# A graph kernel: first gathering in short-format passes, large counts found from the edge list, second root in another space

## The reference, cut to what matters

```python
def rgcn_gate_layer(x, row, col, edge_type, basis, att, gate_w, root, bias):
    w = jnp.einsum('rb,bio->rio', att, basis)          # 2 relations from 30 bases
    x_j = x[col]
    for r in range(2):
        gate = sigmoid(x_j @ gate_w[r, :, 0]); msgs.append(gate[:, None] * x_j @ w[r])
    msg = where(edge_type == 0, msgs[0], msgs[1])
    return segment_sum(msg, row) + x @ root + bias
h   = relu(rgcn_gate_layer(x, ..., basis1, ..., root1, bias1))
out = rgcn_gate_layer(h, ..., basis2, ..., root2, bias2)
```

## Time and profile before

| what | value |
|---|---|
| three timed runs | 1160.33, 1154.93, 1164.74 us; median 1160.33 |
| profiled execution | 1161.15 us; span of its trace 1159.4 us |
| mean granted TensorE clock | 0.985 of full speed |
| busy share of the span | PE 94%, DVE 72%, ACT 48%, POOL 48% |

### The profile page before, as it was taken

The page is one execution under the profiler, slowest core; times in us unless marked ns, Lnnn a source line. Parts: engine busy times, 40 slices in busy tenths (PEclk is TensorE's granted clock), DMA queues, the critical chain, the costliest instruction groups (busy, mean ns, idle before and its releaser), DMA issues. The chain is left out here.

```text
span 1159.4 us, 15448 instructions
## 1 busy us (share of the span) xinstructions
PE 1086.1 (94%) x4410; PEld 607.0 (52%) x4442; DVE 835.8 (72%) x1852; ACT 558.3 (48%) x978; POOL 559.3 (48%) x518
## 2 busy tenths in 40 slices
PE   3989888899999989899999999999999999999997
PEld 1564222344557453655565565555555557446664
DVE  5694677769755153688788788788888867849997
ACT  0221321310332221477777777777777744116663
POOL 1960112233433330667876666666666300027774
PEclk9988989999999999899999999999999999999999
DMA  7995997657211005595554454445454010026665
GB/s 283 341 404 212 360 400 264 231 184 233 84 48 46 13 14 194 132 259 111 114 110 92 101 98 95 100 95 97 98 98 88 1 55 23 9 93 197 203 206 173
DMA packets 60182, 172.66 MB, mean 149 GB/s; under 512 B 12645, under 2 KB 13189, under 8 KB 52552
## 3 DMA queue, kind: packets, MB, share of 16 engines
q0 software_dynamic: 31536, 72.01, 26.6%
q1 hardware_dynamic: 28568, 99.66, 23.4%
HBM read 159.65 MB, written 11.98 MB: 148 GB/s over the span
## 5 line engine op out<-in xcount | busy, mean ns | idle before, releaser
L1664 PE MATMUL PS<-wide,hidT 128*128 128x512 f32 x672 | 302.1, 592 | 2.2 <-DVE hidT L1540 0.4
L705 POOL DMA_INDIRECT rec_scratch<-rec_src,slot_row x84 | 102.5, 1220 | 252.8 <-DMA rec_scratch<-rec_src,slot_row 208.2
L1664 PEld LDWEIGHTS PS<-wide,hidT 128*128 128x128 f32 x672 | 128.6, 191 | 122.8 <-issue 120.5
L1482 POOL DMA_INDIRECT pair_sum<-table_j,counts_rec x84 | 136.7, 1627 | 27.3 <-issue 25.3
L1598 ACT ACTIVATE wide<-PS 128x512 f32<-128x512 f32 x168 | 100.5, 598 | 99.6 <-PE PS L1648 63.5
L1801 POOL DMA_INDIRECT u_space<-table_j,wide x87 | 86.1, 990 | 108.7 <-DMA table_j<-agg_space 81.8
L1474 POOL DMA_INDIRECT pair_sum<-table_i,counts_rec x84 | 89.5, 1066 | 98.9 <-PE PS L1648 59.5
L1603 ACT ACTIVATE wide<-wide,two 128x512 f32<-128x512 f32 x168 | 120.9, 720 | 6.2 <-DVE wide L1533 6.2
L1533 DVE SCALAR_TENSOR_TENSOR wide<-wide 128x512 f32<-128x512 f32 x168 | 116.4, 693 | 5.8
L1491 POOL DMA_INDIRECT rec_scratch<-rec_src,slot_row x84 | 89.5, 1066 | 40.9 <-issue 21.6
L1608 ACT ACTIVATE wide<-wide 128x512 f32<-128x512 f32 x168 | 105.8, 630 | 5.3
(11 more groups left out here) (325 smaller groups left out, 1884.9 us busy)
## 6 DMA issues: line engine op xcount, KB each, us to landing
pieces<-basis_rows SPq DMA_DIRECT2D x56, 1024.0 KB, 7.5
ring<-basis_low SPq DMA_DIRECT2D x30, 256.0 KB, 6.4
w_scratch<-pieces SPq DMA_DIRECT2D x112, 32.0 KB
counts_rec<-rec_scratch SPq DMA_DIRECT2D x1, 2856.0 KB, 9.8
rec_scratch<-rec_src,slot_row POOLq DMA_INDIRECT x168, 2.3
root<-L_gnn_root SPq DMA_DIRECT2D x2, 1024.0 KB, 8.0
rows_in<-in_rows_in SPq DMA_DIRECT2D x2, 1024.0 KB, 13.9
w_rel<-w_scratch SPq DMA_DIRECT2D x1, 2048.0 KB, 11.6
```

The costliest lines, as they stand in the source:

```text
L705: nc.gpsimd.indirect_dma_start(out=rec3_dram, out_offset=bass.IndirectOffsetOnAxis(ap=slot_row[:, 1, t:t + 1], axis=0), in_=rec, in_offset ...
L1482: nc.gpsimd.indirect_dma_start(out=pair_sum[:, t % GOT3, :], out_offset=None, in_=tables[0][1], in_offset=bass.IndirectOffsetOnAxis(ap=idx ...
L1664: m = nc.tensor.matmul(o, hidT[:, t % 2, k * P:(k + 1) * P], w2[:, k, :], start=False, stop=(k == KT - 1), skip_group_check=True)
```

## The change

Four things are done; the diff is cut to its core.

- **The first gathering** takes `counts_short` and two roundings of the gated rows, `first_hi` and `first_lo`, in 100 short multiplications instead of 50 full ones, with `rest` corrections as in the second gathering. ACT rounds the rows (`first_high`) and the counts (`counts_rounded`) during `Y0_LATE`; DVE does `split_block(0)`, `(1)` and `first_low` right after the last `unpack`.
- **The blocks with large counts** are found in the sort stage, from how many edges go from group to group: DVE copies the group marks (`both_kinds`), PE multiplies them (`pair_sums`, `block_sums`), DVE sums them and finds the numbers (`sums_of_groups`, `sums_of_blocks`, both `heavy_blocks`). The maxima over the counts are gone.
- **root2** is loaded into the space of the first weights (`w_rel[0]`), before most of the low blocks, and `root_rows` stands before Y1. `w_ij` goes to the place after Y1.
- **DVE's order**: `records` moves from the count stage to tile 40 of the sort stage; the bias additions and ten `sum2` move before the last `unpack`.

```diff
+            root = pieces[:, 4 * RING1 + 2:4 * RING1 + 2 + KT, :]
+            first_hi = nc.alloc_sbuf_tensor_at("first_hi", [P, 2 * NT, D], F32R, offset=packed_at)
+            root2 = w_rel[0][:, 0, :, :]
+            first_rows = pieces[:, FIRST_SLOT:FIRST_SLOT + 2 * NT, :]
+            first_lo = pieces_short[:, FIRST_SLOT:FIRST_SLOT + 2 * NT, :]
+            FIRST_HIGH_AT = 6
+            ROUNDED_PER = {7: 2, 8: 4, 9: 4}
-            SUM2_BEFORE_H1 = (16, 11, 11, 11, 11)
+            SUM2_EARLY = 10
+            SUM2_BEFORE_H1 = (6, 6, 6, 6, 6)
+            PAIR_SUMS_AT, BLOCK_SUMS_AT = 20, 50
...
 PE:
-                def gathered_first(c):
-                    for m_ in range(NT):
-                        if c == 0:
-                            pe.wait_ge(sem("counts"), 2 * NT + m_ + 1)
-                        for r in range(2):
-                            m = nc.tensor.matmul(PS[:, c, :], counts[r][:, m_, c * P:(c + 1) * P], y_first(r, m_),
-                                                 start=(m_ == 0 and r == 0), stop=(m_ == NT - 1 and r == 1))
-                    m.then_inc(sem("o0_mm"), 1)
+                def gathered_first(c, terms):
+                    for m_, r, part in terms:
+                        pe.wait_ge(sem("counts_short"), 2 * m_ + r + 1)
+                        pe.wait_ge(sem("first_lo" if part is first_lo else "first_hi"), 2 * m_ + r + 1)
+                        m = nc.tensor.matmul(PS[:, c, :], counts_short[r][:, m_, c * P:(c + 1) * P], part[:, first_at(r, m_), :],
+                                             start=((m_, r, part) == FIRST_TERMS[0]), stop=((m_, r, part) == FIRST_TERMS[-1]), skip_group_check=True)
+                    return m
+                def pair_sums():
+                    pe.wait_ge(sem("src_group"), 3)
+                    for g in range(ET // SUM_TILES):
+                        m = nc.tensor.matmul(PS[0:SUM_ROWS, SUMS_BANK, 0:2 * SUM_ROWS]..., dst_group[:, g, :, :]..., src_group[:, :, :, tiles], ...)
+                def block_sums():
+                    pe.wait_ge(sem("group_sums"), 4)
+                    for k in range(NT):
+                        m = nc.tensor.matmul(PS[0:1, SUMS_BANK, 2 * NT * k:2 * NT * (k + 1)], own_group[:, k:k + 1], group_sums, ...)
...
+                pe.wait_ge(sem("heavy_at"), 2)
+                rest_chunk = [rest_numbers(j, 8, NT - 1) for j in range(2)]
+                rest_first = [rest_numbers(j, 12, 2 * NT - 1) for j in range(2)]
                 for n in Y0_LATE:
...
-                    gathered_first(c)
+                pe.wait_ge(sem("rests"), 2)
+                for c in range(NT):
+                    gathered_first(c, FIRST_TERMS[:1])
+                pe.wait_ge(sem("first_hi"), 2 * NT)
+                pe.wait_ge(sem("first_lo"), 2 * NT)
+                for j in range(2):
+                    rest(rests[:, j, :], rest_chunk[j], (first_hi, first_lo), rest_first[j])
+                for c in range(NT):
+                    gathered_first(c, FIRST_TERMS[1:]).then_inc(sem("o0_mm"), 1)
                     if c:
                         pe.wait_ge(sem("h1"), c)
                         turn_rows(c - 1, turn(("T1", c - 1), alone))
                 for c in range(NT):
+                    if c == 0:
+                        pe.wait_ge(sem("root_in"), 32)
+                        for d in range(NT):
+                            if d == 1:
+                                pe.wait_ge(sem("h1"), NT)
+                                turn_rows(NT - 1, turn(("T1", NT - 1), alone))
+                            pe.wait_ge(sem("side_ev"), side["T1", d] + 1)
+                            root_rows(d)
                     gates(1, (c,), turn(("G1", c), alone))
...
-                    if c in HEAVY_AT:
-                        heavy(HEAVY_AT.index(c))
-                pe.wait_ge(sem("root_in"), 32)
-                for c in range(NT):
-                    root_rows(c)
                 pe.wait_ge(sem("y_lo"), 2 * NT)
...
-                    rest(rests[:, j, :], rest_numbers(j, 8, NT - 1), (y_hi, y_lo), rest_numbers(j, 4, 2 * NT - 1))
+                    rest(rests[:, j, :], rest_chunk[j], (y_hi, y_lo), rest_numbers(j, 4, 2 * NT - 1))
 SP:
-                for b in range(RING2, NB):
+                for b in range(RING2, RING2 + SUM2_EARLY // 2):
                     load_low(b)
                 sp.wait_ge(sem("side_mm"), side["Y0", 1, NT - 1] + 1)
-                for r in range(2):
-                    sp.dma_start(w_ij[r], ...).then_inc(sem("w_ij_in"), 16)
-                sp.wait_ge(sem("o0_mm"), NT)
-                sp.dma_start(root[:], w_of("L0_gnn_root2")).then_inc(sem("root_in"), 16)
+                sp.dma_start(root2, w_of("L0_gnn_root2")).then_inc(sem("root_in"), 16)
+                for b in range(RING2 + SUM2_EARLY // 2, NB):
+                    load_low(b)
...
                 sp.wait_ge(sem("side_mm"), side["Y1", 1, NT - 1] + 1)
+                for r in range(2):
+                    sp.dma_start(w_ij[r], ...).then_inc(sem("w_ij_in"), 16)
 DVE:
+                    if e == 10:
+                        both_kinds()
+                    if e == 40:
+                        records()
+                    if e == 44:
+                        sums_of_groups()
+                    if e == 74:
+                        sums_of_blocks()
+                        heavy_blocks(0)
+                        heavy_blocks(1)
...
-                    if t == 6:
-                        records()
...
-                for c in range(NT):
-                    unpack(2, c)
                 dve.wait_ge(sem("att2_in"), 16)
...
                     nc.vector.tensor_tensor(h_rows[:, c, :], h_rows[:, c, :], bias1, ALU.add).then_inc(sem("r0_bias"), 1)
-                done = 0
+                for n in range(SUM2_EARLY):
+                    sum2(n)
+                for c in range(NT):
+                    unpack(2, c)
+                split_block(0)
+                split_block(1)
+                for n in range(2 * NT):
+                    first_low(n)
+                done = SUM2_EARLY
...
-                    if c == 0:
-                        largest(0, 0)
-                        largest(0, 1)
-                        mark_heavy(0)
...
-                heavy_blocks(1)
                 dve.wait_ge(sem("deg"), 1)
                 split_block(2)
                 split_block(3)
 ACT:
+                def first_high(n):
+                    r, c = Y0[n]
+                    at = first_at(r, c)
+                    act.wait_ge(sem("counts"), 3 * NT)
+                    act.wait_ge(sem("side_ev"), side["Y0", r, c] + 1)
+                    nc.scalar.copy(first_hi[:, at, :], first_rows[:, at, :]).then_inc(sem("first_hi"), 1)
+                def counts_rounded(m, r):
+                    act.wait_ge(sem("rests"), 2)
+                    nc.scalar.copy(counts_short[r][:, m, :], counts[r][:, m, :]).then_inc(sem("counts_short"), 1)
                 for n in Y0_LATE:
...
+                    if n == FIRST_HIGH_AT:
+                        for i in range(n + 1):
+                            first_high(i)
+                    if n > FIRST_HIGH_AT:
+                        first_high(n)
+                        for _ in range(ROUNDED_PER[n]):
+                            counts_rounded(*rounded.pop(0))
...
-                for r in range(2):
-                    for m in range(NT):
-                        act.wait_ge(sem("rests"), 2)
-                        nc.scalar.copy(counts_short[r][:, m, :], counts[r][:, m, :]).then_inc(sem("counts_short"), 1)
```

More of the change, by code:

```diff
@@ L237, in gnn_stack @@
             group_id = part(10)
-            values = part(11)[:, 0:ET]
+            values = part(11)
             by_chunk = part(12).rearrange("p (j t) -> p j t", j=4)
@@ new lines, in sums_of_blocks @@
+                def sums_of_blocks():
+                    by_block = PS[0:1, SUMS_BANK, 0:2 * NT * NT].rearrange("p (k q n) -> p k q n", k=NT, q=2)
+                    total, first, second = (f.rearrange("p (k n) -> p k n", k=NT) for f in
+                                            (found_of[1], found_of[0][:, 0:NT * NT], found_of[0][:, NT * NT:2 * NT * NT]))
+                    dve.wait_ge(sem("block_sums"), 1)
+                    dve.wait_ge(sem("rec_set"), 2)
+                    nc.vector.tensor_copy(total, by_block[:, :, 0, :]).then_inc(sem("found"), 1)
+                    nc.vector.tensor_copy(second, by_block[:, :, 1, :]).then_inc(sem("found"), 1)
+                    dve.wait_ge(sem("found"), 2)
+                    nc.vector.tensor_tensor(first, total, second, ALU.subtract).then_inc(sem("found"), 1)
+                    dve.wait_ge(sem("found"), 3)
@@ L1189, in _ @@
+                    for j in range(2):
+                        b = dve.value_load(heavy_at[0:1, 16 + j:17 + j], min_val=0, max_val=NT * NT - 1)
+                        block = blocks[1][:, bass.ds(b, 1), :].rearrange("p b n -> p (b n)")
```

(18 more changed lines are left out.)

224 lines of the change are left out of this document (128 added, 96 removed).

## The result

The changed kernel takes 1149.7 us (median; 1146.2 to 1156.3), the kernel before 1160.7 beside it. The ratio is 0.9911, interval 0.9895 to 0.9926: 10.3 us less, or 11.0 by the medians. 1148.0 was predicted. The profiled execution took 1147.3 us, span 1145.5, so 13.9 us less than the profiled one of before.

The account below looks back on a forecast made before the run. PE was taken as the bound, busy throughout from 240.0 to 366.4 us. Terms -19.7 + 2.1 + 2.0 + 3.2 - 0.2 + 0.3 = -12.3 us gave 1148.0 us; range 1141 to 1157.

Parts of the forecast that it names:

- Short passes: First gathering: 100 short multiplications (23.4 us) replace 50 full ones (43.1 us), 19.7 us less.
- Later begin: First gathering: PE stands 0.8 us for the last row's rounding and subtraction, then corrections take 1.3; together 2.1 us more.
- Register loads: Four loads on PE ahead of the last products at 207: 2.0 us more, bounds nothing and 2.7.
- root_rows moved: Before the second gathering: uncovered wait for Y1's last low part 2.2 us, register loads 1.0; 3.2 us more.
- DVE just in time: Before Y1: DVE's low blocks end 1.1 us before PE needs them at 287.4; 0.3 us for h1 waits.
- Scatters: Before the third layer: must end at least 7.3 us earlier; 10.8 us expected, slack 3.5 us.
- Up to the second gathering: PE's summed gain, 12.3 us less, with that gathering beginning near 330 instead of 342.7.
- Rival 3: Stall before the second gathering lowers PE's clock: price up to 6.3 us, 1148 to 1154; chance 0.13.
- Rival 2: Sort stage: PE's gap shrinks and the clock stays, up to 6.3 us more gain, 1142; chance 0.10.

Follow-up runs that it names:

- the kernel before with early records: Kernel before the change, with only records moved to tile 40 of the sort stage: 1160.6 us, ratio 1.0017.
- covered stall: Changed kernel with the second gathering's first 16 multiplications put ahead of the wait for the last low parts: 1145.5 us, ratio 0.9871.
- the loads moved: Changed kernel with its four register loads moved from ahead of the late Y0 products to the end of the sort stage: 1146.6 us, ratio 0.9891.
- the scatters held: Changed kernel with the scatters held until the count stage has counted six tiles: 1158.3 us, ratio 0.998.
- both without low passes: Changed kernel without 49 of the first gathering's 50 low passes: with pair slots after the table readouts 1154.9 us; with half the low blocks instead 1143.8 us.
- root_rows behind Y1: Changed kernel with root_rows put back behind the Y1 products, root2 still loaded early: 1162.8 us, ratio 1.0024.
- the stall in the kernel before: Kernel before the change, with root_rows put between the fourth and fifth blocks' Y1 products: 1173.7 us, ratio 1.0118.
- GCN loads moved: Changed kernel with only the GCN layer's four register loads moved ahead of its wait for x1: 1149.9 us, ratio 0.991.
- both versions with all of it: Changed kernel with loads moved, stalls covered, pair slots and blank DMA moved: all ten loads at sort stage's end 1144.0 us; only four there 1138.7 us.

## Why the prediction was right, and where not

- **Short passes** (-19.7). Right: 26.26 us, less 0.84 of stall, 1.02 of corrections and 3 x 0.43 of transposes, is 23.1 for the 100; 23.4 was said. The two waits in front of each cost nothing, as taken.
- **Later begin** (+2.1): 0.84 + 1.02 = 1.9.
- **Register loads** (+2.0): 2.61. Shown by moving them: the gap goes whole. In the seven profiles that keep them behind the counting it is 2.52 to 2.81. The Trainium skill ("TensorE: Matmul & The Clock Gate", section on the array's architecture) gives TensorE a queue 64 deep. That the loads would therefore run ahead was the prediction's own reading, weighed and not taken; these gaps show that they did not.
- **root_rows moved** (+3.2): 2.90 + 0.18 = 3.1. The split holds, too: DVE's last low part ends 2.1 us behind the last product (325.86 against 323.77), and 0.8 and 0.18 are left for the wake-up and the register loads, 0.1 and 1.0 said. It stayed that short only because ACT's rounding of the counts had moved as well; the prediction names that move, but not that root_rows had covered the rounding. Left behind Y1, it made a stall of 9.23 us in the kernel before.
- **DVE just in time**: 1.1 us of slack was said, 1.8 found, and 0.3 for `h1` was not needed. (The gates take 0.81 us; the prediction's own division gives 1.1 for them, not the 0.9 that it uses.) Without the low passes nothing more came from PE's side there, but what holds first is `h1` behind the load of a low block, not the last low block.
- **Scatters**: the last is issued 10.2 us earlier (10.8 said), `rec` is there 10.4 earlier, and the slack is 2.5 (3.5 said). Needed: shown from both sides.
- **Up to the second gathering** this makes 12.15 us from the counting on (328.14 against 342.73, each less its end of counting); 12.3 was said.
- **Missed: the clock in the GCN layer.** Of the 12.15 us, 10.4 are left at the next phase. 1.3 us went in the 24 multiplications and 0.4 in the correction ahead of them, which together is nearly the difference. The median lies 1.7 us above the forecast, which fits it. Rival 3, that the stall takes the clock, was given 0.13 and placed at the stall, at a price of up to 6.3 us. In the changed kernel's profile it came behind two more gaps 70 us later; in four other kernels with such a stall the clock fell right behind it, as the rival had it (last section).
- **Rival 2, the sort stage's clock**, is neither shown nor excluded. The gap did shrink, from 2.79 to 1.03 us, and where those gates ran, from 80 to 92 us, the clock was 0.50 before and 0.72 after. But counting began at 105.6 before, at 103.7 after, at 104.3 in the kernel before with early records, and anywhere from 100.6 to 106.4 in variants of the changed kernel with the same sort stage.

## What to carry to other kernels

Work that is moved has covers at both ends: look for everything that hid under it at its old place (here a rounding on another engine and a low part), and put some of the next stage's own work there before its last input arrives. When one engine gets 20 us faster in a stage, first list the chains that end just behind it; here two had to move along, and each alone would have taken back most of the gain. Small reads into registers belong where the engine waits anyway, in portions that fit that wait.

## What was not expected of the hardware

The stall and the clock go together over a long distance. Ten of the thirteen kernels have the two gaps of 1.4 and 1.0 us in front of the GCN layer's 24 multiplications. In three of these PE has no gap of 2.9 us or more between 255 and 355 us (before, before with early records, covered stall), and the 24 took 5.60 to 5.61 us. In seven it has one (the changed kernel, the loads moved, the scatters held, both without low passes, root_rows behind Y1, the stall in the kernel before), and they took 6.6 to 7.3. Where the two gaps were gone they took 5.60 to 5.63, with the stall (GCN loads moved) or without it (both versions with all of it). So those small gaps alone don't lower the clock (the kernel before has them at 1.00), and with an earlier stall they do.

The stall can also take the clock at once. Of the seven kernels that have one right in front of the second gathering, three ran its first 60 multiplications in 13.8 us at 1.00 (the changed kernel and both without low passes). Four took 14.4 to 15.4 us at a granted clock of 0.95 to 0.89 (the loads moved, the scatters held, the stall in the kernel before, the GCN loads moved), and all of these but the last were slow at the 24 again. Every kernel has one profile, so how often one and the same kernel shows the lower clock at either place is not known, and why the stall can show only behind later gaps stays open. The Trainium skill (same page, Part 1) says that the gate's watching runs free of the program, so that one kernel may show it at different places; no run here tests that. The price was 1.0 to 1.7 us at the 24 and 0.6 to 1.6 in the second gathering, on top of the stall.
